# Distances in ScalarE's pauses, grid ahead of the second norm, experts ahead of the x transposes, another order of loads

## The chip, the cores and the metric

One core of a Trainium2 chip. The metric is the device time of one execution in microseconds. Three runs of the kernel before took 381.7, 383.23 and 385.96 us (median 383.23). Engines in this text: TensorE (PE; its weight loads PEld), VectorE (DVE), ScalarE (ACT), GpSimd (POOL) and SyncE (SP), which here only issues DMAs.

## The reference

Input x is 16 images of 256 tokens with 128 channels, in float32. Cut to what matters:

```
mod = silu(c) @ wmod                       # 16 x 6 x 128: sa, ca, ga, sb, cb, gb per image
h   = layernorm(x) * (1 + ca) + sa
# deformable attention: per token 8 heads x 33 taps
wave   = silu(h @ wave_w.T + wave_b)       # gives a frequency and a phase per token
w      = silu(h @ kernel_w.T + kernel_b)   # 8 heads x 33 weights
pos    = clip(l + s * freq + phase, 0, 255)          # s = -16 .. 16
out    = sum_s w[s] * (linear interpolation of h at pos[s])
x   = x + ga * silu(out @ out_w.T)
h   = layernorm(x) * (1 + cb) + sb
# experts: the two best of 8 by h @ router_w.T + router_b, not weighted
x   = x + gb * (sum of the two chosen experts' h @ expert_w[e] + expert_b[e])
```

The gates ga and gb are kept at least 0.25 away from zero.

## The kernel before, in words

The 16 images are cut into nine units: image 0 alone, seven units of two images, image 15 alone. A unit of two images is four tiles of 128 tokens. Each engine has its program written out by hand: a loop over i = -2 to 7, in which each pass works on several units at once, and after it a hand-written tail for the last two units (LATE is unit 7, LAST is unit 8). Engines meet only through semaphores; each engine runs its list strictly in order.

One pass i does this:

- **front of unit i+1**. ScalarE normalises x (norm1, one pass earlier), TensorE transposes it (front_xT), ScalarE applies the modulation (front_hT), TensorE multiplies with the 297 projection columns (front_row), ScalarE writes silu into the table T (front_row) and takes two tanh (front_wave). VectorE turns these into a line per token (`line`, L616 to L624) and into the weights of the ends (`ends_of`, `products`). ScalarE spreads the line over 50 grid columns (front_u, L422 and L429), and VectorE makes from it the shift masks and `near`, the distance of each grid column from its tap (`grid`, L648 to L660).
- **middle of unit i**. VectorE shifts T by six predicated copies (`network`, L673). ScalarE turns `near` into the interpolation weights c: six Abs of 172 columns each, one for each offset within a block (front_c, L439), then one Relu (L442). VectorE multiplies T by c into the dense attention matrix AT (`spread_out`, L705, two instructions for each image). TensorE transposes AT in 8 groups for each image (mid_A, L879), ScalarE copies each group out of PSUM (mid_A, L453), and TensorE multiplies with h (mid_attend, L893). The second image of unit i gets its mid_A in the next pass. Then come aoT, the output projection, silu, gate, and VectorE adds to x (`residual`, L724).
- **back of unit i-1**. ScalarE sums squares (stats2, L348), GpSimd makes the reciprocal root in three small dependent operations (rstd2, L306, L308, L310), ScalarE normalises (norm2, L362), TensorE transposes (back_x2T, L919), ScalarE modulates (back_h2T, L484), TensorE makes logits (L929), VectorE picks the two best (`route`, L733 to L749), and the masks go out to DRAM and come back spread over all partitions (two DMAs of SyncE).
- **end of unit i-2**. VectorE multiplies h by the masks (`masked`, L766, one instruction an image), TensorE multiplies with the 8 experts (back_experts, L967, one call an image), ScalarE scales (back_moe, L500), TensorE transposes back, VectorE adds to x (`total`), SyncE stores.

What sets the order around the change is the list of each engine. ScalarE's runs: front_hT, mid_A of the second image, mid_ao, mid_y, mid_gate, the rows of T, front_wave, front_hs, front_c, stats2, norm2, front_u, back_h2T, back_moe, mid_A of the first image, back_mk, norm1 (L503 to L521). VectorE's runs: network 0 and 1, stats1, sum_ends, network 2 and 3, masked of image 0, network 4, masked of image 1, residual, network 5, line, ends_of, spread_out of image 0, grid, route, spread_out of image 1, products, total (L776 to L799). TensorE's is at L976 to L998: there the first image's experts are multiplied ahead of the transposes of x, and the second image's behind them.

At the start ScalarE's queue issues cT, the whole of wmod, the biases and the projection weights, SyncE's queue the rest. VectorE splits the biases into three bf16 parts and sums them on three partitions (parts_on_partitions), then copies all modulation out of PSUM.

## Time and profile before

| | |
|---|---|
| median of three runs | 383.23 us (381.7 to 385.96) |
| the profiled execution's own time | 380.88 us |
| its span, first to last instruction | 379.1 us |
| PE busy | 269.6 us (71%) |
| PEld busy | 185.9 us (49%) |
| DVE busy | 287.3 us (76%) |
| ACT busy | 218.4 us (58%) |
| POOL busy | 55.8 us (15%) |
| mean granted TensorE clock | 0.86 of full speed |
| DMA | 12.91 MB, mean 34 GB/s |

The profiled execution is 2.35 us below the median of the three runs, and its own time is 1.78 us above its span. Busy shares are averages over a start (to 38.2 us), seven long passes of the loop (to 320.05 us) and a tail (59.05 us); the stretches are cut where VectorE begins the shifts of a unit.

### The profile page before, as it was taken

The page shows a single profiled execution, that of the slowest core. Times are in us where ns is not written, and L with a number is a line of the kernel's source. Part 1 is how long each engine was busy: PE and PEld are TensorE (multiplying, and loading weights), DVE is VectorE, ACT ScalarE, POOL GpSimd, SP SyncE. Part 2 cuts the span into 40 slices and gives each one's busy share as a digit, 9 for nine tenths or more (in the row PEclk, how much of TensorE's full clock was granted, in tenths as well). Part 3 has the DMA queues.
Part 4 walks back from the last instruction along what each step waited for, and adds up shares of the span by engine and source line. Part 5 has one row for each costly group of instructions (what it writes and reads, how often), then busy time and mean ns, then how long its engine had stood idle before and what let it go on. Part 6 is the DMA issues. An engine that isn't in the chain of part 4 may idle for free.

```text
span 379.1 us, 5072 instructions
## 1 busy us (share of the span) xinstructions
PE 269.6 (71%) x1720; PEld 185.9 (49%) x1720; DVE 287.3 (76%) x650; ACT 218.4 (58%) x539; POOL 55.8 (15%) x64
## 2 busy tenths in 40 slices
PE   6745815894598749890988639892898388779796
PEld 2324404543464537560764427551664266357574
DVE  6699996997499846997299954998299949950723
ACT  2573665856576846774486744854576546565301
POOL 5110231112102030205002140114000300001100
PEclk9686975999589969997699958997699979889889
DMA  7600000200012000400022000400013002200001
GB/s 223 160 2 0 2 0 0 58 0 0 3 27 100 0 1 2 139 3 0 0 83 59 0 0 2 141 2 0 1 44 97 1 2 56 85 0 3 28 0 42
DMA packets 11871, 12.91 MB, mean 34 GB/s; under 512 B 1139, under 2 KB 10694, under 8 KB 11078
## 3 DMA queue, kind: packets, MB, share of 16 engines
q1 hardware_dynamic: 11108, 12.05, 10.6%
q10 hardware_dynamic: 738, 0.55, 0.6%
q8 instruction: 13, 0.21, 0.2%
q14 instruction: 12, 0.10, 0.1%
HBM read 10.45 MB, written 2.15 MB: 33 GB/s over the span
## 4 chain that ended last, share of the span: by engine, by line
PE 47%; ACT 27%; DVE 10%; POOL 8%; issue 7%; DMA 1%; SPq 0%; ACTq 0%; POOLq 0%; DVEq 0%
PE pT L879 12%; PE pE L967 12%; ACT A L453 6%; PE pR L859 5%; POOL rs L308 5%; ACT xn L362 5%; PE pY L893 4%; ACT c L439 4%; DVE T L673 3%; ACT xn L348 3%; DVE AT L705 2%; PE pL L929 2%; PE pY L903 2%; POOL ve L306 2%; ACT hT L383 2%
## 5 line engine op out<-in xcount | busy, mean ns | idle before, releaser
L879 PE MATMUL pT<-early,AT 128*128 128x128 f32 x512 | 78.6, 301 | 21.9 <-ACT A L453 11.6
L453 ACT ACTIVATE A<-pT 128x512 f32<-128x512 f32 x128 | 71.2, 596 | 30.2 <-PE pT L879 30.2
L673 DVE COPY_PREDICATED T<-mask,T 128x672 f32<-128x672 int16 (+11 forms) x54 | 82.9, 1534 | 1.0
L879 PEld LDWEIGHTS pT<-early,AT 128*128 128x128 f32 x512 | 61.3, 154 | 36.8 <-ACT A L453 23.6
L705 DVE TENSOR_TENSOR AT<-T,c 128x2064 f32<-128x2064 f32 x32 | 72.3, 2302 | 2.8 <-ACT c L442 2.8
L967 PE MATMUL pE<-hm,late 128*128 128x256 f32 x240 | 66.8, 440 | 0.0
L967 PEld LDWEIGHTS pE<-hm,late 128*128 128x128 f32 x240 | 52.3, 224 | 10.9 <-issue 1.3
L306 POOL TENSOR_SCALAR ve<-sq 128x4 f32<-128x4 f32 (+1 forms) x18 | 9.7, 538 | 295.0 <-ACT xn L348 159.0
L919 PE MATMUL pX<-early,xn 128*128 128x128 f32 x32 | 8.4, 407 | 62.1 <-ACT xn L362 62.1
L362 ACT ACTIVATE xn<-x,nm,rs 128x128 f32<-128x128 f32 x64 | 26.4, 480 | 34.9 <-POOL nm L310 34.9
L919 PEld LDWEIGHTS pX<-early,xn 128*128 128x128 f32 x32 | 5.3, 202 | 65.1 <-ACT xn L362 65.0
L893 PE MATMUL pY<-A,hs 128*32 128x256 f32 x512 | 32.2, 394 | 0.0
L766 DVE TENSOR_TENSOR hm<-mkb,h2T 128x2048 f32<-128x2048 bf16 x13 | 29.6, 2278 | 0.0
L308 POOL TENSOR_TENSOR rs<-ve,mhalf 128x4 f32<-128x4 f32 (+1 forms) x18 | 28.9, 1603 | 1.5
L859 PE MATMUL pR<-proj,hT 128*128 128x297 f32 x64 | 25.7, 485 | 0.8 <-ACT hT L383 0.8
L500 ACT ACTIVATE moeT<-pE,modT 128x256 f32<-128x256 f32 x15 | 6.3, 471 | 28.2 <-PE pE L967 28.2
L648 DVE SCALAR_TENSOR_TENSOR eI<-uR,early 128x200 int16<-128x200 f32 (+1 forms) x9 | 3.1, 344 | 24.6 <-ACT uR L429 24.4
L893 PEld LDWEIGHTS pY<-A,hs 128*32 128x32 f32 x512 | 15.4, 113 | 12.3 <-ACT A L453 3.1
L395 ACT ACTIVATE T<-pR 128x297 f32<-128x297 f32 x32 | 13.6, 424 | 13.4 <-PE pR L859 13.4
L439 ACT ACTIVATE c<-near,early 128x172 f32<-128x172 f32 (+1 forms) x54 | 20.1, 542 | 0.0
L733 DVE TENSOR_TENSOR lg<-pL,rb 128x32 f32<-128x32 f32 (+1 forms) x9 | 1.7, 187 | 23.3 <-PE pL L929 23.2
L724 DVE SCALAR_TENSOR_TENSOR x<-pY,x 128x128 f32<-128x128 f32 x32 | 7.5, 289 | 14.7 <-PE pY L909 14.7
(129 smaller groups left out, 359.4 us busy)
## 6 DMA issues: line engine op xcount, KB each, us to landing
mkb<-mask_rows SPq DMA_DIRECT2D x6, 1024.0 KB, 5.2
x<-in_x SPq DMA_DIRECT2D x7, 256.0 KB, 7.5
out<-x SPq DMA_DIRECT2D x7, 256.0 KB, 5.0
late<-in_late SPq DMA_DIRECT2D x1, 592.0 KB, 5.5
mkb<-mask_rows SPq DMA_DIRECT2D x1, 512.0 KB, 5.1
wmod<-in_wmod ACTq DMA_DIRECT2D x1, 384.0 KB, 4.1
early<-in_early SPq DMA_DIRECT2D x1, 278.0 KB, 4.3
x<-in_x SPq DMA_DIRECT2D x2, 128.0 KB, 3.6
```

What stands on the lines that cost most here:

```text
L306: nc.gpsimd.tensor_scalar(ve[:, 0:w], sq[:, 0:w], 1.0 / C, EPS, ALU.mult, ALU.add).then_inc(done, 1)
L308: nc.gpsimd.tensor_tensor(rs[:, 0:w], ve[:, 0:w], mhalf[:, 0:w], ALU.pow).then_inc(out, 1)
L362: ins = nc.scalar.activation(xn[:, bt, :], of_x(n)[:, bt, :], ACT.Identity, bias=nm[:, bt:bt + 1], scale=rs[:, bt:bt + 1])
L439: ins = nc.scalar.activation(cells[:, :, :, r], near[:, 0:w, :], ACT.Abs, bias=off[:, r:r + 1])
L453: nc.scalar.activation(A[b][:, m, 2 * j:2 * j + 2, :].rearrange("p h l -> p (h l)"), pT[k % 2][:, :], ACT.Copy).then_inc(a_A, 1)
L673: nc.vector.copy_predicated(rows[:, :, :, j0:j1], spread(mask[:, k, 0:w, j0:j1], [P, w, H, j1 - j0], 2), rows[:, :, :, j0 + (1 << bit):j1 ...
L705: nc.vector.tensor_tensor(AT[:, bt, :, :].rearrange("p h (j r) -> p h j r", r=BLK), spread(T[n % 2][:, bt, 0:H, 0:NB], [P, H, NB, BLK], 3) ...
L766: nc.vector.tensor_tensor(hm[b][:, :, :], mkb[n % 2][:, :, b * L:(b + 1) * L], spread(own, [P, E, L], 1), ALU.mult).then_inc(v_hm, 1)
L859: mm(dst, hT[:, bt * P:(bt + 1) * P], proj[:, :], start=False, stop=True).then_inc(t_row, 1)
L879: ins = nc.tensor.transpose(pT[k % 2][:, c0:c0 + P], AT[:, 2 * b + i, 2 * j + a, m * P:(m + 1) * P], ident)
L893: ins = mm(pY[32 * j:32 * j + 32, b * L:(b + 1) * L], hs[n % 2][:, 2 * b + m, hh, :], A[b][:, m, hh, :], start=(m == 0 and a == 0), stop=( ...
L967: ins = mm(dst, weT[:, e, :], hm[b][:, e, :], start=False, stop=(e == E - 1))
```

## The change

- ScalarE: front_c is cut into its six Abs, which go one, one, one and three at a time between the pieces of the front and of the middle, and the Relu (front_fall) between the last two rows of T. The second image's mid_A moves ahead of front_hT, stats2 ahead of front_hs, and front_u ahead of norm2.
- TensorE: the first half of the second image's mid_A moves ahead of front_xT; front_row comes between the pieces of the middle; the second image's experts move ahead of back_x2T.
- VectorE: residual moves ahead of the second masked; the expert biases are prepared one pass earlier, the gates one pass later.
- Start: ident gets a load of its own, the projection weights move to SyncE's queue, wmod comes in two parts and so does the modulation; the loads of x from unit 2 on and of the late weights wait until the first front_hT has run.
- Tail: the lists of all engines are ordered anew; the first image's masked of unit 6 goes ahead of spread_out of unit 8, and its experts ahead of mid_gate of unit 7.

The diff, cut to its core:

```diff
@@ -259,13 +260,20 @@
                 sp.dma_start(of_x(n), rows_of("x", n)).then_inc(d_x[n], 16)
 
             load_x(0)
+            sp.dma_start(packs["first"][:, :], t["first"]).then_inc(d_first, 16)
+            sp.dma_start(proj[:, 0:NW], t["proj"][:, 0:NW]).then_inc(d_proj, 16)
+            sp.dma_start(proj[:, NW:NW + H], t["proj"][:, NW:NW + H]).then_inc(d_proj, 16)
+            sp.dma_start(proj[:, NW + H:NW + 2 * H], t["proj"][:, NW + 32:NW + 40]).then_inc(d_proj, 16)
+            load_x(1)
             sp.dma_start(packs["early"][:, :], t["early"]).then_inc(d_early, 16)
             sp.dma_start(bits[:, :, :], t["bits"].rearrange("p (k j) -> p k j", j=NGRID)).then_inc(d_bits, 16)
-            load_x(1)
             sp.dma_start(packs["experts"][:, :], t["experts"]).then_inc(d_exp, 16)
+
+            sp.wait_ge(a_hT, 1)
+            load_x(2)
             sp.dma_start(packs["late"][:, :], t["late"]).then_inc(d_late, 16)
             sp.dma_start(rb[:, :], t["rb"].rearrange("(a e) -> a e", a=1).to_broadcast([P, E])).then_inc(d_late, 16)
-            for n in range(2, NU):
+            for n in range(3, NU):
                 load_x(n)
 
             def masks(n):
...
@@ -328,16 +336,14 @@
         @block.scalar
         def _(act):
             act.dma_start(cT[:, :], t["cT"]).then_inc(d_c, 16)
-            act.dma_start(wmod[:, :], t["wmod"]).then_inc(d_wmod, 16)
+            act.dma_start(wmod[:, 0:2 * C], t["wmod"][:, 0:2 * C]).then_inc(d_wmod[0], 16)
             act.dma_start(kbl[:, 0:NW], t["kbl"].to_broadcast([NP, NW])).then_inc(d_kb, 16)
             wvb = t["wvb"].rearrange("r a -> a r")
             act.dma_start(kbl[:, NW:NW + H], wvb[:, 0:H].to_broadcast([NP, H])).then_inc(d_kb, 16)
             act.dma_start(kbl[:, NW + H:NW + 2 * H], wvb[:, 32:32 + H].to_broadcast([NP, H])).then_inc(d_kb, 16)
             act.wait_ge(d_c, 16)
             nc.scalar.activation(scT[:, :], cT[:, :], ACT.Silu).then_inc(a_silc, 1)
-            act.dma_start(proj[:, 0:NW], t["proj"][:, 0:NW]).then_inc(d_proj, 16)
-            act.dma_start(proj[:, NW:NW + H], t["proj"][:, NW:NW + H]).then_inc(d_proj, 16)
-            act.dma_start(proj[:, NW + H:NW + 2 * H], t["proj"][:, NW + 32:NW + 40]).then_inc(d_proj, 16)
+            act.dma_start(wmod[:, 2 * C:6 * C], t["wmod"][:, 2 * C:6 * C]).then_inc(d_wmod[1], 16)
 
             def squares(n, junk, total, mu, meant, count, sq, done):
 
...
@@ -428,17 +434,21 @@
                     act.wait_ge(v_sc, n)
                 nc.scalar.activation(uR[:, 0:tiles(n), :], u[:, 0:tiles(n), :], ACT.Copy, bias=ROUND).then_inc(a_uR, 1)
 
-            def front_c(n):
+            def front_c(n, r0, r1):
 
                 w = tiles(n)
-                act.wait_ge(v_near, n + 1)
-                if n > 0:
-                    act.wait_ge(v_mult, LT * before(n))
+                if r0 == 0:
+                    act.wait_ge(v_near, n + 1)
+                    if n > 0:
+                        act.wait_ge(v_mult, LT * before(n))
                 cells = c[:, 0:w, :].rearrange("p a (j r) -> p a j r", r=BLK)
-                for r in range(BLK):
-                    ins = nc.scalar.activation(cells[:, :, :, r], near[:, 0:w, :], ACT.Abs, bias=off[:, r:r + 1])
-                ins.then_inc(a_abs, 1)
-                act.wait_ge(a_abs, n + 1)
+                for r in range(r0, r1):
+                    nc.scalar.activation(cells[:, :, :, r], near[:, 0:w, :], ACT.Abs, bias=off[:, r:r + 1]).then_inc(a_abs, 1)
+
+            def front_fall(n):
+
+                w = tiles(n)
+                act.wait_ge(a_abs, BLK * (n + 1))
                 nc.scalar.activation(c[:, 0:w, :], c[:, 0:w, :], ACT.Relu, bias=1.0, scale=-1.0).then_inc(a_c, 1)
 
             def mid_A(n, b, halves=(0, 1)):
...
@@ -501,41 +513,47 @@
                                          scale=scale_of(5, n, b)).then_inc(a_moe, 1)
 
             for i in range(-2, LAST):
+                second(i, -1, mid_A, 1)
                 run(i, 1, front_hT)
-                second(i, -1, mid_A, 1)
+                run(i, 0, front_c, 0, 1)
                 run(i, -1, mid_ao)
+                run(i, 0, front_c, 1, 2)
+                run(i, 1, front_row, 0)
+                run(i, 0, front_c, 2, 3)
                 run(i, -1, mid_y)
                 run(i, -1, mid_gate)
-                run(i, 1, front_row, 0)
                 run(i, 1, front_row, 1)
+                run(i, 0, front_c, 3, BLK)
+                run(i, 1, front_row, 2)
+                run(i, 0, front_fall)
+                run(i, 1, front_row, 3)
                 run(i, 1, front_wave)
+                run(i, -1, stats2)
                 run(i, 1, front_hs)
-                run(i, 0, front_c)
-                run(i, -1, stats2)
+                run(i, 1, front_u)
                 run(i, -1, norm2)
-                run(i, 1, front_u)
                 run(i, -1, back_h2T)
                 run(i, -2, back_moe)
                 run(i, 0, mid_A, 0)
                 run(i, -1, back_mk)
                 run(i, 2, norm1)
-            mid_A(LATE, 1, (0,))
-            front_c(LAST)
-            mid_A(LATE, 1, (1,))
+            mid_A(LATE, 1)
+            front_c(LAST, 0, BLK)
             mid_ao(LATE)
+            front_fall(LAST)
             mid_y(LATE)
             mid_gate(LATE)
             mid_A(LAST, 0)
             stats2(LATE)
             mid_ao(LAST)
-            norm2(LATE)
             mid_y(LAST)
             mid_gate(LAST)
+            norm2(LATE)
             back_h2T(LATE)
             back_moe(LATE - 1)
             stats2(LAST)
+            norm2(LAST)
             back_mk(LATE)
-            norm2(LAST)
             back_h2T(LAST)
             back_mk(LAST)
             back_moe(LATE)
...
@@ -566,25 +588,35 @@
                 nc.vector.memset(T[0][:, :, :, :], 0.0).then_inc(v_zero, 1)
 
             def projection_parts():
-                dve.wait_ge(d_early, 16)
                 dve.wait_ge(d_kb, 48)
                 dve.wait_ge(g_zero, 3)
-                parts_on_partitions(kbl[:, :], kbr[:, :], kbs, kbt, kbp[:, :], ident[0:NP, 0:NP], v_kbp)
+                parts_of(kbl[:, :], kbr[:, :], kbs, v_kbp)
+
+            def projection_rows():
+                dve.wait_ge(d_first, 16)
+                on_partitions(kbs, kbt, kbp[:, :], ident[0:NP, 0:NP], v_kbp)
 
             def expert_parts():
                 dve.wait_ge(d_exp, 16)
-                parts_on_partitions(eb, ebr[:, :], ebs, ebt, ebp[:, :], pmask, v_ebp)
+                parts_of(eb, ebr[:, :], ebs, v_ebp)
+                on_partitions(ebs, ebt, ebp[:, :], pmask, v_ebp)
+
+            def selectors():
                 nc.vector.tensor_copy(sel[:, :, :], spread(ident[0:NP * E, 0:E], [NP * E, E, P], 2)).then_inc(v_ebp, 1)
 
-            def modulation():
-                dve.wait_ge(t_mod, 1)
-                nc.vector.tensor_copy(modT[:, :, :].rearrange("p k b -> p (k b)"), pR[0][:, 0:6 * B]).then_inc(v_modT, 1)
-                dve.wait_ge(v_modT, 1)
-                nc.vector.tensor_scalar(modT[:, 1:5:3, :], modT[:, 1:5:3, :], 1.0, None, ALU.add).then_inc(v_modT, 1)
+            def modulation(part):
+
+                ks = slice(0, 2) if part == 0 else slice(2, 6)
+                dve.wait_ge(t_mod, part + 1)
+                nc.vector.tensor_copy(modT[:, ks, :].rearrange("p k b -> p (k b)"),
+                                      pL[:, ks.start * B:ks.stop * B]).then_inc(v_modT, 1)
+                dve.wait_ge(v_modT, 2 * part + 1)
+                nc.vector.tensor_scalar(modT[:, 3 * part + 1, :], modT[:, 3 * part + 1, :], 1.0, None, ALU.add).then_inc(v_modT, 1)
 
             def gates():
 
                 gate = modT[:, 2:6:3, :]
+                dve.wait_ge(v_modT, 3)
                 nc.vector.tensor_scalar(gsT[:, :, :], gate, 0.0, 2.0, ALU.is_ge, ALU.mult)
                 nc.vector.scalar_tensor_tensor(gaT[:, :, :], gate, -1.0, gate, ALU.mult, ALU.max).then_inc(v_gate, 1)
                 dve.wait_ge(v_gate, 1)
...
@@ -773,19 +807,21 @@
                                         ALU.add).then_inc(v_out, 1)
 
             start()
-            for i in range(-2, LAST):
+            stats1(0)
+            projection_parts()
+            modulation(0)
+            projection_rows()
+            for i in range(-1, LAST):
                 run(i, 0, network, range(0, 2))
                 run(i, 2, stats1)
-                if i == -2:
-                    projection_parts()
-                    modulation()
-                    gates()
+                if i == -1:
+                    expert_parts()
                 run(i, 0, sum_ends)
                 run(i, 0, network, range(2, 4))
                 run(i, -2, masked, 0)
                 run(i, 0, network, range(4, 5))
+                run(i, -1, residual)
                 second(i, -2, masked, 1)
-                run(i, -1, residual)
                 run(i, 0, network, range(5, 6))
                 run(i, 1, line)
                 run(i, 1, ends_of)
...
@@ -796,11 +832,13 @@
                 run(i, 1, products)
                 run(i, -2, total)
                 if i == 0:
-                    expert_parts()
+                    modulation(1)
+                    gates()
+                    selectors()
             network(LAST, range(0, 6))
             sum_ends(LAST)
+            masked(LATE - 1, 0)
             spread_out(LAST, 0)
-            masked(LATE - 1, 0)
             residual(LATE)
             masked(LATE - 1, 1)
             residual(LAST)
...
@@ -825,11 +863,14 @@
             pe.wait_ge(v_zero, 1)
             warm_up(9)
             pe.wait_ge(a_silc, 1)
-            pe.wait_ge(d_wmod, 16)
-            for k in range(6):
-                ins = mm(pR[0][:, k * B:(k + 1) * B], wmod[:, k * C:(k + 1) * C], scT[:, :], start=True, stop=True)
-            ins.then_inc(t_mod, 1)
-            pe.wait_ge(d_early, 16)
+            def modulation(part, ks):
+                pe.wait_ge(d_wmod[part], 16)
+                for k in ks:
+                    ins = mm(pL[:, k * B:(k + 1) * B], wmod[:, k * C:(k + 1) * C], scT[:, :], start=True, stop=True)
+                ins.then_inc(t_mod, 1)
+
+            modulation(0, range(0, 2))
+            pe.wait_ge(d_first, 16)
 
             def front_xT(n):
                 pe.wait_ge(a_xn1, n + 1)
...
@@ -974,21 +1015,24 @@
                 ins.then_inc(t_out, 1)
 
             for i in range(-2, LAST):
+                second(i, -1, mid_A, 1, 0)
                 run(i, 1, front_xT)
-                second(i, -1, mid_A, 1, 0)
                 second(i, -1, mid_A, 1, 1)
                 second(i, -1, mid_attend, 1, 0)
                 second(i, -1, mid_attend, 1, 1)
+                run(i, 1, front_row, 0)
                 run(i, -1, mid_y)
-                run(i, 1, front_row, 0)
+                run(i, 1, front_row, 1)
                 run(i, -1, mid_gate)
-                run(i, 1, front_row, 1)
+                run(i, 1, front_row, 2, 3)
+                if i == -1:
+                    modulation(1, range(2, 6))
                 run(i, 1, front_hb)
                 if i == -1:
                     warm_up(9)
                 run(i, -2, back_experts, 0)
+                second(i, -2, back_experts, 1)
                 run(i, -1, back_x2T)
-                second(i, -2, back_experts, 1)
                 run(i, -1, back_logits)
                 run(i, 0, mid_A, 0, 0)
                 run(i, -2, back_out)
```

The hunks left out declare the semaphores, make back_h2T and back_logits of unit 0 wait for the second part of the modulation, split parts_on_partitions into parts_of and on_partitions, move the wait for `early` to line(0), and reorder TensorE's tail: there back_experts(LATE - 1, 0) moves from behind mid_attend(LAST, 0, 1) to between mid_y(LATE) and mid_gate(LATE), and back_experts(LATE - 1, 1) from behind back_x2T(LATE) to before it.

## Rows read from the trace of the kernel before

**Rows 1.** Busy us by stretch: length, PE, PEld, DVE, ACT, POOL, granted clock, DMA share, GB/s.

```profile
196.96:240.80 43.84, 31.71 (x210) 22.26 (x209) 34.11 (x75) 26.47 (x66) 7.64 (x6) 0.84 0.09 30
...
320.05:379.10 59.05, 47.60 (x277) 34.06 (x274) 28.91 (x67) 24.28 (x60) 2.70 (x6) 0.88 0.11 34
```

**Rows 2.** VectorE's waits between 38.2 and 320.05: us in total, times, longest.

```profile
DVE eI L648 <- ACT uR L429: 24.0, 6, 4.2
DVE lg L733 <- PE pL L929: 22.9, 6, 5.1
DVE AT L705 <- ACT c L442: 2.8, 2, 2.0
```

**Rows 3.** Order of time, VectorE, one pass: start, us, instruction, idle before in brackets.

```profile
209.86 2.28 DVE L766 TENSOR_TENSOR hm<-mkb,h2T 128x2048 f32<-128x2048 bf16 x1
...
212.90 1.80 DVE L673 COPY_PREDICATED T<-mask,T 128x1376 f32<-128x1376 int16 x1
...
215.31 0.16 DVE L624 SCALAR_TENSOR_TENSOR nlf<-lp,invf 128x4 f32<-128x4 f32 x1
...
216.39 4.52 DVE L705 TENSOR_TENSOR AT<-T,c 128x2064 f32<-128x2064 f32 x2
...
225.45 0.37 DVE L648 SCALAR_TENSOR_TENSOR eI<-uR,early 128x200 int16<-128x200 f32 x1 [4.18 <-ACT uR L429]
...
232.29 0.19 DVE L733 TENSOR_TENSOR lg<-pL,rb 128x32 f32<-128x32 f32 x1 [5.00 <-PE pL L929]
```

**Rows 4.** Order of time, ScalarE, the same pass.

```profile
211.55 2.40 ACT L439 ACTIVATE c<-near,early 128x172 f32<-128x172 f32 x6
213.98 1.06 ACT L442 ACTIVATE c<-c 128x1032 f32<-128x1032 f32 x1
...
222.09 1.65 ACT L362 ACTIVATE xn<-x,nm,rs 128x128 f32<-128x128 f32 x4 [5.28 <-POOL nm L310]
223.64 1.37 ACT L422 ACTIVATE u<-early,nlf,invf 128x50 f32<-128x50 f32 x4
...
225.32 1.00 ACT L484 ACTIVATE h2T<-pX,modT 128x256 f32<-128x256 f32 x2
...
232.84 1.09 ACT L453 ACTIVATE A<-pT 128x512 f32<-128x512 f32 x2 [0.44 <-PE pT L879]
...
238.35 1.63 ACT L362 ACTIVATE xn<-x,nm,rs 128x128 f32<-128x128 f32 x4
```

**Rows 5.** Order of time, TensorE, the same pass.

```profile
210.71 3.72 PE L967 MATMUL pE<-hm,late 128*128 128x256 f32 x16
223.79 1.12 PE L919 MATMUL pX<-early,xn 128*128 128x128 f32 x4 [9.36 <-ACT xn L362]
...
225.16 6.30 PE L967 MATMUL pE<-hm,late 128*128 128x256 f32 x16
231.30 0.95 PE L929 MATMUL pL<-late,h2T 128*128 128x8 f32 x8
```

**Rows 6.** Order of time, GpSimd, that pass and a later one.

```profile
216.97 1.77 POOL L306 TENSOR_SCALAR ve<-sq 128x4 f32<-128x4 f32 x1 [12.72 <-ACT xn L348]
218.83 2.95 POOL L308 TENSOR_TENSOR rs<-ve,mhalf 128x4 f32<-128x4 f32 x1
...
299.90 1.10 POOL L308 TENSOR_TENSOR rs<-ve,mhalf 128x4 f32<-128x4 f32 x1
```

**Rows 7.** VectorE's waits up to 38.2.

```profile
DVE kbs L548 <- DMA early<-in_early: 1.7, 1, 1.7
```

**Rows 8.** Order of time, ScalarE, the start.

```profile
9.74 0.56 ACT L383 ACTIVATE hT<-pX,modT 128x256 f32<-128x256 f32 x1 [2.65 <-DVE modT L583]
```

**Rows 9.** Order of time, VectorE, the start: first of eight operations for expert biases.

```profile
35.66 0.21 DVE L548 CAST ebs<-experts 24x128 bf16<-24x128 f32 x1
```

**Rows 10.** Order of time, ScalarE, the tail.

```profile
354.44 0.59 ACT L493 ACTIVATE mkT<-pL 24x512 bf16<-24x512 f32 x1 [1.77 <-PE pL L935]
```

**Rows 11.** Order of time, VectorE, the first spread_out of a later pass.

```profile
300.63 4.52 DVE L705 TENSOR_TENSOR AT<-T,c 128x2064 f32<-128x2064 f32 x2
```

More of the change, by code:

```diff
@@ L74 @@
 PACKS = {
-    "early": (P, [("ident", P), ("xrow", NGRID), ("jcol", BT * NGRID), ("off", BLK), ("ends", BT * 2 * END),
+    "first": (P, [("ident", P)]),
+    "early": (P, [("xrow", NGRID), ("jcol", BT * NGRID), ("off", BLK), ("ends", BT * 2 * END),
                   ("sign", BT * 2), ("edge", BT * 2), ("lcol", BT)]),
@@ L167, in build @@
         pL = bank("pL")
[L169 removed]
+        d_c = sem("d_c"); d_wmod = [sem(f"d_wmod{i}") for i in range(2)]; d_first = sem("d_first"); d_early = sem("d_early"); d_late = sem("d_late"); d_kb = sem("d_kb")
         d_proj = sem("d_proj"); d_bits = sem("d_bits"); d_exp = sem("d_exp")
@@ L384, in front_hT, with front_row @@
                                          bias=scale_of(0, n, b), scale=scale_of(1, n, b)).then_inc(a_hT, 1)
-            def front_row(n, b):
-                for bt in range(LT * b, min(LT * (b + 1), tiles(n))):
+            def front_row(n, *own):
+                for bt in (q for q in own if q < tiles(n)):
                     g = LT * before(n) + bt
@@ L545, in _, with parts_of @@
         def _(dve):
-            def parts_on_partitions(x_, rest, parts, sums_, out, of_part, done):
+            def parts_of(x_, rest, parts, done):
                 nc.vector.tensor_copy(parts[:, 0, :], x_).then_inc(done, 1)
@@ L842, in front_xT, with front_row @@
                 ins.then_inc(t_xT, 1)
-            def front_row(n, b):
-                for bt in range(LT * b, min(LT * (b + 1), tiles(n))):
+            def front_row(n, *own):
+                for bt in (q for q in own if q < tiles(n)):
                     g = LT * before(n) + bt
                     if g == 0:
-                        pe.wait_ge(v_modT, 1)
                         pe.wait_ge(v_kbp, 7)
@@ L1003, in _ @@
             mid_y(LATE)
+            back_experts(LATE - 1, 0)
             mid_gate(LATE)
```

13 lines of the change are left out of this document (9 added, 4 removed).

## The prediction

> **What bounds the kernel now.** I first cut the span where VectorE starts the shifts of a unit. A full pass of the loop takes 43.84 us and holds 34.11 us of VectorE, 31.71 of TensorE and 26.47 of ScalarE [rows 1]. No engine is full, so the order is the bound. VectorE's waits show where: between 38.2 and 320.05 us it waited 24.0 us for uR, 22.9 for the logits and 2.8 for c [rows 2], 49.7 us in all. The order of time in one pass shows why: VectorE runs without a gap from the start of the pass at 196.96 to the end of the first spread_out near 221.3 (225.45 less the wait), waits 4.18 us for the grid's input and, 1.84 us of grid later (232.29 - 5.00 - 225.45), 5.00 us for the logits [rows 3]. The line `nlf` that ScalarE needs for the grid is ready at 215.47 [rows 3], but ScalarE stands in norm2 and waits for GpSimd until 222.09; u and its rounding run from 223.64 to 225.32 [rows 4]. So the grid waits for a norm that it does not need. The logits wait for the same norm (x transposes at 223.79, behind 9.36 us of idle TensorE) and then for the second image's experts, 6.30 us between the x transposes and the logits [rows 5].
>
> GpSimd is late for two reasons. Its chain starts only at 216.97, since ScalarE does the six Abs (2.40 us) and the Relu (1.06) first [rows 4, 6]. And its small operations stand still while VectorE runs a large one: `ve` took 1.77 us from inside the first AT product, `rs` 2.95 from inside the second, ending 0.9 us after it; an `rs` that began at 299.90, among VectorE's small operations, took 1.10 [rows 3, 6].
>
> **The loop, step by step**, in the clock times of this pass, with VectorE unbroken from 196.96.
>
> *Residual* ran in the 0.76 us between the end of the second masked (212.14) and network 5 (212.90) [rows 3]. Ahead of masked, which takes 2.28, it ends near 210.7. VectorE's sum is unchanged, and `nlf` stays at 215.5. ScalarE's stats2 took from the Relu's end (215.04) to 216.97, so 1.9 us [rows 4, 6]; it now ends near 212.6 if ScalarE is free.
>
> *The Abs and the Relu* add no work: 3.46 us move. Their cover is ScalarE's waits in the first half. Of its 17.4 us without work (43.84 - 26.47 [rows 1]) 5.28 lie before norm2 [rows 4] and about as much behind the experts, at most 6.30 [rows 5]; some 6 remain for attend, output projection and rows, and I take 3 of them as usable. That covers most; what isn't covered delays the second tanh by at most 1 us against a need of `line` near 214.6. If the cover is gone the cost is 3.46 us on ScalarE, not on VectorE. front_hT moves into the wait for attend.
>
> *GpSimd.* `ve` then stands in masked (to 212.9 in the new order), `rs` in network 5 (to 214.7) and ends 0.9 us later at 215.6; nm is there at 216. It must begin before the AT products at 216.39, or it waits for the first of them (2.3 us).
>
> *u ahead of norm2*: 215.5 to 217.2 (1.68 us). *norm2* 217.2 to 218.85. The second image's *experts*: masked ends at 212.9, so the two calls (3.72 us each after busy stretches [rows 5]) end by 220 at worst and, by the start of the first call at about 211, by 218.7. *x transposes* 0.7 to 1.1, *h2T* 1.0, *logits* 0.95 at most [rows 4, 5]: they end between 221.4 and 222.
>
> *VectorE*: the grid follows the first spread_out at 221.3, with its input four microseconds old, so no wait. The route is due at 223.1, with logits 1 to 1.7 us before it: no wait. The pass becomes 43.84 - 4.18 - 5.00 = 34.66 us, VectorE's own 34.11 plus its issue gaps. Late next would be the logits; then ScalarE: from its first copy of A (232.84) to the end of norm1 (239.98) are 7.14 us [rows 4]. The first copy now comes at about 222.6 (behind logits), so norm1 ends at 229.8, just as the second spread_out ends; the next copies need that and 0.7 us more. ScalarE has 0.7 us to spare there, and 3 us at the residual. SyncE's mask transfers start earlier with mkT and are no nearer to their user.
>
> Over the loop the waits of 49.7 us go, at most. I give back 3 us for places where a unit's slack runs out (seven passes at 0.4): **-47**. Bounds: none of the small slacks holds, 14 us given back; or nothing given back.
>
> **The start.** VectorE waited 1.7 us for `early` before the bias parts [rows 7], and ScalarE's first hT waited 2.65 us for the modulation behind them [rows 8]. Now the parts need only the biases, the modulation comes in between, and the sums after it. hT gains up to 2.65. The first projection still follows all seven bias operations and now two of the modulation too, at 0.2 us each (the smallest in [rows 3] are 0.16 and 0.19): 1.7 - 0.4, about 1.2. The projection's loads leave SyncE's queue earlier but now share the first microseconds with fewer bytes of wmod. From 0 (loads land no earlier) to 2.5. The expert biases (seven operations, with the selectors' one from 35.66 to 38.2, 2.5 us [rows 9]) move ahead of the first line, where VectorE has nothing else. At the mean of 0.32 us the seven are 2.2; six small ones of modulation and gates, put at 0.2 to 0.3 each, take their place: 0.7 us gained. The held back loads of x are needed 10 us after their issue; cost nothing, or, if unit 2 lands late, 2 us. Sum **-2**, from +1 to -3.5.
>
> **The tail** (59.05 us [rows 1]). A call of 16 expert products, 3.72 us at the full clock [rows 5], leaves the stretch between the last attend and the x transposes of unit 7. Against that, mid_gate of unit 7 waits for the first of them (2.3 us later than it could), and the last spread_out comes behind a masked (2.28 us); since ScalarE's copies of unit 7 are no longer split by front_c, the last transposes still start about 1 us earlier. norm2(LAST) ahead of back_mk(LATE) costs 0.8 us. Walking the lists, mkT of unit 7 comes 3 us earlier than its 354.44 - 320.05 = 34.4 us after the stretch begins [rows 10]; behind it nothing changes. **-3**, from +1 to -6.
>
> Sum: 380.88 - 47 - 2 - 3 = 328.9 us for an execution like the profiled one. The median lay 2.35 us above it: **331 us**.
>
> **A rule against it.** The rows show that GpSimd waits for VectorE's large two-input instructions. They show no wait the other way: the AT products at 300.63 began while `rs` of 299.90 ran, and took 4.52 us like those of [rows 3] [rows 6, 11]. The Trainium skill (SBUF — State Buffer, "SBUF: two separate sides") calls the pair of ports that the two share an exclusive lock: whichever instruction starts first has it whole, and the other blocks. By that rule VectorE, now unbroken, would stand for each GpSimd operation that slips in first.
>
> **Rivals.**
> (a) *The small slacks fail*: nm misses 216.39, or the logits come 1 to 2 us late, in each of seven passes: 7 to 14 us back, 335 to 345. For: nm has 0.2 to 0.4 us. Against: even nm at 218.9 moves the logits to 223.5 only. 0.17.
> (b) *GpSimd is shut out*: if `rs` is let in neither behind masked nor behind network 5, it ends after the first spread_out, near 222. norm2 ends at 224, the logits at 227 with slower transposes: VectorE waits 4 us in each of 7 passes, 28 less the 3 given back: 356. Against: `ve` of 216.97 was let in between two back-to-back products [rows 6]. 0.06.
> (c) *VectorE stands for GpSimd*: an exclusive hold would cost VectorE three operations of 0.2, 1.0 and 0.2 us a pass, 1.4 x 7 = 10 us: 341. This is what the rule quoted above would do here. Against it stand the products at 300.63 [rows 11]. 0.05.
> (d) *Slower: TensorE's granted clock.* A pass holds 31.71 us of TensorE at 0.84 of the full clock [rows 1], 26.6 at full. It is not granted fully, and drops after idle stretches (3.72 us against 6.30 for the same products [rows 5]). If work packed closer were granted less, TensorE would be the bound: at 1.2 GHz (0.5) a pass would be 53 us, 9.4 more than now in each of seven: 449. It decides against the change below 26.6 / 43.84 = 0.61. Against: the tail, busy for 47.60 of 59.05 us, was granted 0.88, the pass, busy for 31.71 of 43.84, 0.84 [rows 1]. 0.02.
> (e) *It does more*: nothing given back and a better clock in the tail, 320 to 324. 0.07.
> (f) *It doesn't do what it says*: ScalarE, now with 0.7 us to spare, becomes the bound and its copies of A start late, about 4 us a pass: 356, like (b). 0.04.
>
> **How the numbers follow.** My forecast (324 to 336) has 0.59. 331 is its middle, a little to the late side. The range 322 to 345 leaves out (b), (f), (d) and half of (e), and half of (c) may stand at its edge; some 0.83 is in it. A change under 1% could not be told from none in this kernel. All cases but (d) lie over 1% below 383.23, so faster 0.96; for a cause that I do not see, both others get the rest: same 0.02, slower 0.02.
>
> **What would show it.** Right: passes of 34.5 to 35.5 us; no entry of VectorE for uR or logits over 1 us in total a pass; u ahead of norm2's end; the second experts at 3.7 us, not 6.3; `rs` ending near 18.7 us after the pass begins. Wrong: VectorE's wait at lg of 2 us or more (a, b); AT products or shifts longer than 4.52 and 1.80 us (c); TensorE rows at 1.5 times their length throughout (d); waits of TensorE for A copies that stand behind norm1 (f).

## The result: 327 us, the loop shorter by 48.7 us

The changed kernel took 326.8 us (median of four runs, 326.45 to 327.7) against 383.26 for the one before (four runs): a ratio of 0.8524, 95% interval 0.8473 to 0.8575. The profiled execution took 327.7 us, with a span of 325.9. The forecast was 331.

| | before | after |
|---|---|---|
| span of the profiled execution | 379.1 us | 325.9 us |
| start, to VectorE's first shift of unit 1 | 38.20 | 36.12 |
| loop, seven passes | 281.85 | 233.16 |
| tail | 59.05 | 56.62 |
| a middle pass | 43.84 | 34.5 |
| VectorE busy | 287.3 (76%) | 286.1 (88%) |
| TensorE busy | 269.6 (71%) | 266.9 (82%) |
| mean granted clock | 0.86 | 0.895 |

The engines do the same work; what went is idle time. One pass of the changed kernel and its tail, cut as in [rows 1], with the same columns:

```profile
169.08:203.64 34.56, 30.29 (x196) 22.15 (x200) 33.96 (x74) 25.58 (x64) 5.75 (x6) 0.90 0.13 38
...
269.28:325.90 56.62, 46.28 (x285) 32.84 (x281) 29.01 (x67) 23.65 (x60) 2.52 (x6) 0.91 0.12 35
```

A pass of 34.56 us holds 33.96 of VectorE: it is now the bound. The granted clock rose with the packing, 0.84 in [rows 1] and 0.90 here. What is left of VectorE's waits, over the whole span (us in total, times, longest):

```profile
DVE x L758 <- PE pY L949: 10.1, 1, 10.1
DVE hm L794 <- PE pT L987: 9.2, 3, 4.6
DVE lg L767 <- PE pL L970: 4.1, 3, 1.6
...
DVE eI L682 <- ACT uR L435: 0.8, 1, 0.8
```

The entry for uR, 24.0 us in [rows 2], is 0.8, once, in the start. Of the 4.1 us for the logits, 22.9 in [rows 2], only 1.6 lie in the loop. The large ones left, x and hm, lie in the tail, as they did before.

One pass of the changed kernel, which begins at 169.08, in order of time. VectorE:

```profile
185.06 1.81 DVE L707 COPY_PREDICATED T<-mask,T 128x1376 f32<-128x1376 int16 x1
...
188.61 4.52 DVE L739 TENSOR_TENSOR AT<-T,c 128x2064 f32<-128x2064 f32 x2
...
193.39 0.36 DVE L682 SCALAR_TENSOR_TENSOR eI<-uR,early 128x200 int16<-128x200 f32 x1
...
195.14 0.18 DVE L767 TENSOR_TENSOR lg<-pL,rb 128x32 f32<-128x32 f32 x1
```

No bracket stands behind eI (4.18 us in [rows 3]) nor behind lg (5.00). ScalarE:

```profile
180.38 1.05 ACT L452 ACTIVATE c<-c 128x1032 f32<-128x1032 f32 x1
...
187.70 1.38 ACT L428 ACTIVATE u<-early,nlf,invf 128x50 f32<-128x50 f32 x4 [2.33 <-DVE nlf L658]
...
189.39 1.63 ACT L368 ACTIVATE xn<-x,nm,rs 128x128 f32<-128x128 f32 x4
191.77 1.02 ACT L496 ACTIVATE h2T<-pX,modT 128x256 f32<-128x256 f32 x2 [0.75 <-PE pX L959]
```

The Relu is done 12.4 us into the pass (18.1 in [rows 4]), u comes before norm2, and norm2 no longer waits 5.28 us for GpSimd. GpSimd:

```profile
185.05 1.84 POOL L314 TENSOR_SCALAR ve<-sq 128x4 f32<-128x4 f32 x1 [8.64 <-ACT xn L354]
186.97 1.01 POOL L316 TENSOR_TENSOR rs<-ve,mhalf 128x4 f32<-128x4 f32 x1
188.06 0.20 POOL L318 TENSOR_TENSOR nm<-mu,rs 128x4 f32<-128x4 f32 x1
```

`ve` was held up (1.84 us) by the shift of 185.06, `rs` ran free at 1.01 where [rows 6] had 2.95. `nm` ends at 188.26, 0.35 us before the first AT product at 188.61. TensorE:

```profile
185.43 3.72 PE L1008 MATMUL pE<-hm,late 128*128 128x256 f32 x16
191.08 0.66 PE L959 MATMUL pX<-first,xn 128*128 128x128 f32 x4 [1.93 <-ACT xn L368]
192.85 1.40 PE L970 MATMUL pL<-late,h2T 128*128 128x8 f32 x8 [1.11 <-ACT h2T L496]
194.10 3.81 PE L919 MATMUL pT<-first,AT 128*128 128x128 f32 x16
```

The second experts are finished before the x transposes, at 3.72 us and not the 6.30 of [rows 5], and the x transposes wait 1.93 us and not 9.36. The low clock has not gone, it has moved: the 16 transposes of A behind the logits were granted 0.50 and took 3.81 us, where the kernel before needed 1.07 to 1.14 for eight of them (at 232.11 and 233.49). VectorE waits for none of them.

Not every pass had that 0.35 us. In the second of the seven, which begins at 66.37, `rs` started only 0.04 us before the AT products, and `nm` met the first of them:

```profile
83.58 1.01 POOL L316 TENSOR_TENSOR rs<-ve,mhalf 128x4 f32<-128x4 f32 x1
84.67 1.33 POOL L318 TENSOR_TENSOR nm<-mu,rs 128x4 f32<-128x4 f32 x1
```

```profile
83.62 4.53 DVE L739 TENSOR_TENSOR AT<-T,c 128x2064 f32<-128x2064 f32 x2
...
91.87 0.19 DVE L767 TENSOR_TENSOR lg<-pL,rb 128x32 f32<-128x32 f32 x1 [1.62 <-PE pL L970]
```

`nm` ended 2.38 us after the products began, and the logits came 1.62 us late: this is the 1.6 us of the loop.

Start and tail, each by a ScalarE row of the changed kernel: the first hT, which came at 9.74 after 2.65 us of waiting [rows 8], and mkT of unit 7, which came 34.4 us after the tail's beginning [rows 10] and now 31.8.

```profile
8.14 0.56 ACT L389 ACTIVATE hT<-pX,modT 128x256 f32<-128x256 f32 x1 [0.65 <-PE pX L882]
```

```profile
301.07 0.59 ACT L505 ACTIVATE mkT<-pL 24x512 bf16<-24x512 f32 x1 [0.15 <-PE pL L976]
```

### The profile page after: what moved, and what is told of

Read it like the earlier page. It is cut to its first block, busy times and chain, and to the rows that moved or that the text cites. A ratio compares the mean times of both kernels' runs of the same rounds, so it can differ in the third digit from the quotient of the medians.

```text
span 325.9 us, 5078 instructions
## 1 busy us (share of the span) xinstructions
PE 266.9 (82%) x1720; PEld 185.7 (57%) x1720; DVE 286.1 (88%) x652; ACT 217.6 (67%) x539; POOL 44.0 (13%) x64
## 4 chain that ended last, share of the span: by engine, by line
DVE 48%; PE 23%; issue 16%; ACT 10%; POOL 2%; ACTq 0%; DVEq 0%; POOLq 0%
DVE T L707 14%; DVE AT L739 13%; PE pT L919 7%; DVE hm L800 4%; PE pE L1008 4%; ACT A L463 3%; PE pR L899 2%; PE pL L970 2%; ACT xn L368 1%; DVE prodN L719 1%; DVE x L758 1%; DVE topi L775 1%; DVE endw L727 1%; PE pY L933 1%; DVE st L632 1%
## 5 line engine op out<-in xcount | busy, mean ns | idle before, releaser
L919 PE MATMUL pT<-first,AT 128*128 128x128 f32 x512 | 83.3, 316 | 18.2 <-DVE AT L749 10.6
L919 PEld LDWEIGHTS pT<-first,AT 128*128 128x128 f32 x512 | 66.0, 162 | 34.4 <-ACT A L463 17.2
L1008 PE MATMUL pE<-hm,late 128*128 128x256 f32 x240 | 57.4, 394 | 0.0
L1008 PEld LDWEIGHTS pE<-hm,late 128*128 128x128 f32 x240 | 45.5, 195 | 7.8 <-issue 0.2
L316 POOL TENSOR_TENSOR rs<-ve,mhalf 128x4 f32<-128x4 f32 (+1 forms) x18 | 19.9, 1104 | 1.5
L428 ACT ACTIVATE u<-early,nlf,invf 128x50 f32<-128x50 f32 x32 | 11.2, 417 | 11.3 <-DVE nlf L658 11.3
L959 PE MATMUL pX<-first,xn 128*128 128x128 f32 x32 | 6.3, 320 | 13.8 <-ACT xn L368 13.8
L970 PE MATMUL pL<-late,h2T 128*128 128x8 f32 x60 | 9.6, 285 | 8.3 <-ACT h2T L496 8.3
L970 PEld LDWEIGHTS pL<-late,h2T 128*128 128x128 f32 x60 | 8.9, 225 | 10.5 <-ACT h2T L496 9.4
L318 POOL TENSOR_TENSOR nm<-mu,rs 128x4 f32<-128x4 f32 (+1 forms) x18 | 14.3, 797 | 1.4
```

The source lines that it names most:

```text
L316: nc.gpsimd.tensor_tensor(rs[:, 0:w], ve[:, 0:w], mhalf[:, 0:w], ALU.pow).then_inc(out, 1)
L919: ins = nc.tensor.transpose(pT[k % 2][:, c0:c0 + P], AT[:, 2 * b + i, 2 * j + a, m * P:(m + 1) * P], ident)
L970: ins = mm(pL[:, bt * E:(bt + 1) * E], h2T_of(n)[:, bt * P:(bt + 1) * P], rwT, start=True, stop=True)
L1008: ins = mm(dst, weT[:, e, :], hm[b][:, e, :], start=False, stop=(e == E - 1))
```

## The experiments

Twelve kernels ran. The same 383 us kernel stood beside them each time, at medians of 383.9 to 385.1; ratios are to it.

**The two exchanges alone, on the kernel before.** First ScalarE's u ahead of norm2:

```
# ScalarE's loop
+    run(i, 1, front_u)
     run(i, -1, norm2)
-    run(i, 1, front_u)
```

> The kernel before with one exchange: ScalarE's u (grid input) ahead of norm2. Theory (the order of one pass): u then fits into ScalarE's wait for GpSimd, so VectorE's wait of 4.18 us for uR goes, but the logits come when they came (norm2 still starts with nm, the second experts still stand between the x transposes and the logits), so the wait for the logits grows by as much: about 9 us a pass, total unchanged, 380 to 385 us. Rival (each wait has its own worth): 24 us less, 359.

Measured: 385.64 us, ratio 1.0017 (0.9964 to 1.0069). VectorE's waits in this kernel:

```profile
DVE lg L733 <- PE pL L929: 48.8, 9, 9.4
```

The wait for uR is gone (0.5 us left) and the whole of it has come back at the logits: 48.8 us over the whole span, 47.5 of them in the loop, where [rows 2] had 22.9. Two waits in a row for one cause, the late norm2, and taking away the first pays nothing.

Then the second image's experts ahead of the x transposes:

```
# TensorE's loop
+    second(i, -2, back_experts, 1)
     run(i, -1, back_x2T)
-    second(i, -2, back_experts, 1)
```

> The kernel before with one exchange: the second image's experts ahead of the x transposes on TensorE. Theory: the experts then run in TensorE's 9.4 us of idleness, logits follow h2T by 1 us, near 227.3 in the pass that began at 196.96, just when the grid ends: the wait for the logits falls from 22.9 to under 5 us in all, the wait for uR stays at 24; 361 us (359 to 365). Rival: the logits are held by the norm, not by the experts; under 5 us gained.

Measured: 376.38 us, 0.9781 (0.972 to 0.9843): faster by 7.6 us, a third of the gain that I expected. VectorE's waits, TensorE's order in one pass, and the stretches from its x transposes on (columns as in [rows 1]):

```profile
DVE eI L648 <- ACT uR L429: 27.9, 8, 4.2
...
DVE AT L705 <- ACT c L442: 9.1, 7, 2.0
```

```profile
216.56 3.72 PE L967 MATMUL pE<-hm,late 128*128 128x256 f32 x16
224.50 1.01 PE L919 MATMUL pX<-early,xn 128*128 128x128 f32 x4 [4.21 <-ACT xn L362]
227.09 1.88 PE L929 MATMUL pL<-late,h2T 128*128 128x8 f32 x8 [1.58 <-ACT h2T L484]
228.82 3.81 PE L879 MATMUL pT<-early,AT 128*128 128x128 f32 x16
```

```profile
224.50:228.80 4.30, 2.72 (x12) 2.32 (x13) 1.80 (x5) 3.23 (x9) 0.00 (x0) 0.52 0.01 4
228.80:232.60 3.80, 3.80 (x18) 3.43 (x19) 3.46 (x16) 1.79 (x3) 0.00 (x0) 0.50 0.00 0
```

The experts shrink to 3.72 us, as expected. But TensorE then stands for 4.21 us before the x transposes and is granted 0.52 and 0.50 behind them, the lower of its levels: x transposes 1.01 us (0.66 in the changed kernel), logits 1.88 (1.40), the A transposes 3.81 (as in the changed kernel). In the order before, the experts stood behind the x transposes and were the ones to run slowly in that place [rows 5]. And the AT products now wait for c: ScalarE's copies of A follow the slow transposes, so that its list comes to hT 2.3 us after this pass begins (198.89 and 196.57), where in the kernel before the two fell together (196.89 and 196.96), and the Relu ends 20.4 us into the pass, 18.1 before. In the loop, 15.9 of the 22.9 us at the logits went, but uR took back 3.4 (27.4 and 24.0) and c 5.3 (8.1 and 2.8).

Both together:

> The kernel before with both exchanges, nothing else. Theory: uR in time, logits near 226 against a need at 223.1: 2.9 us of wait a pass are left, 6.3 go; 343 us (339 to 347). If the early GpSimd chain of the changed kernel were not needed at all: 335 or less. Rival (each alone adds up, and u alone is worth 0): as the experts alone, 361.

Measured: 375.47 us, 0.9748 (0.9665 to 0.9831); I had expected 343. The view shows why. GpSimd's chain and ScalarE's norm2 in one pass:

```profile
216.11 0.52 POOL L306 TENSOR_SCALAR ve<-sq 128x4 f32<-128x4 f32 x1 [14.95 <-ACT xn L348]
216.71 2.95 POOL L308 TENSOR_TENSOR rs<-ve,mhalf 128x4 f32<-128x4 f32 x1
219.74 0.59 POOL L310 TENSOR_TENSOR nm<-mu,rs 128x4 f32<-128x4 f32 x1
```

```profile
220.36 1.65 ACT L362 ACTIVATE xn<-x,nm,rs 128x128 f32<-128x128 f32 x4 [2.73 <-POOL nm L310]
```

norm2 still waits for `nm`, and the logits come 5.31 us late in the middle passes: of the 49.7 us of [rows 2], 41.8 are left, 34.4 at the logits and 7.4 at c. The exchanges remove what stands behind the norm, not what makes the norm late. They are worth 8 us without the rest of the change.

**The rest of the change without the exchanges.** In the changed kernel both are undone:

```
# ScalarE's loop
+    run(i, -1, norm2)
     run(i, 1, front_u)
-    run(i, -1, norm2)
# TensorE's loop
+    run(i, -1, back_x2T)
     second(i, -2, back_experts, 1)
-    run(i, -1, back_x2T)
```

> The changed kernel with both exchanges undone (u behind norm2, second experts behind the x transposes); Abs spread, residual early, new start and tail kept. Theory: nm now comes 19 us after the pass begins, norm2 to 20.6, u to 22.4, before the grid is due at 24.3: no wait for uR. x transposes at 20.7, experts to 25.1, logits 26.1, due at 26.1: 0 to 1 us a pass. 327 to 334 us. Rival (the two exchanges carry the gain): 370 or more.

Measured: 343.68 us, 0.8897 (0.8812 to 0.8982), between the two. TensorE's order in one pass and its experts' stretch:

```profile
196.97 1.11 PE L959 MATMUL pX<-first,xn 128*128 128x128 f32 x4 [4.68 <-ACT xn L368]
...
198.33 5.84 PE L1008 MATMUL pE<-hm,late 128*128 128x256 f32 x16
204.01 0.95 PE L970 MATMUL pL<-late,h2T 128*128 128x8 f32 x8
```

```profile
198.33:204.00 5.67, 5.67 (x17) 4.68 (x17) 3.80 (x9) 1.17 (x3) 0.00 (x0) 0.62 0.01 3
```

Spreading the distances, the early residual, start and tail bring some 40 us by themselves. GpSimd is in time in all passes of two-image units but one (there `rs` took 2.95 us and uR came 4.17 us late). The rest hangs on the experts: behind 4.68 us of idle TensorE they are granted 0.62 and take 5.84 us, where I had counted 3.72; the logits come 2.80 us late. Each exchange undone alone tells the two apart:

> The changed kernel with the second image's experts behind the x transposes again. Theory, with the lower clock counted this time: TensorE idles for 5.9 us before the x transposes (22 us after the pass begins), which then take 1.1, the experts 5.8, the logits 0.9: 30 against a need at 26.1, some 4 us of wait a pass, 27 in all: 350 to 356. That is slower than the kernel with both exchanges undone (343.7), since there norm2 doesn't wait for u. Rival (the experts' products at 3.72, as I priced them before): 335. Rival (worth what it was alone in the kernel before, 2.2%): 334.

Experts behind, u ahead: 344.31 us, 0.896 (0.8888 to 0.9032), below the 350 to 356 that I expected. The logits come 1.57 us late in the second pass and 2.75 to 4.35 in the five behind it. The exchange of the experts is worth 17.5 us here. The time is the same as with both undone, so u without the experts gains nothing; the kernel with both undone even had its one pass with a late `rs`, and its other passes were up to 1.5 us shorter than here.

> The changed kernel with u behind norm2 again. Theory: once GpSimd's chain is early (nm 19.2 us after the pass begins), norm2 and u both end 22.5 us after it, before the grid is due at 24.3; nothing is late. 326 to 329 us. Rival (u ahead of norm2 took VectorE's wait for uR away by itself): 20 us slower or more, 347.

u behind, experts ahead: 330.89 us, 0.8621 (0.8553 to 0.869). The profiled execution (329.22) shows five passes of the changed kernel's length, one shorter by 1.25 us, and behind it one of 36.3 (33.7 there), in which `rs` was caught:

```profile
82.62 3.10 POOL L316 TENSOR_TENSOR rs<-ve,mhalf 128x4 f32<-128x4 f32 x1
```

```profile
82.56 4.52 DVE L739 TENSOR_TENSOR AT<-T,c 128x2064 f32<-128x2064 f32 x2
```

It is the same second pass in which the changed kernel's `rs` had started 0.04 us before the products; here it started 0.06 us behind their start, and VectorE waited 3.09 us for uR and 1.00 for the logits. The median is 4 us above the changed kernel's, the profile explains 1.5 of them, and the intervals overlap: what u ahead of norm2 is worth stays open between nothing and 4 us.

**What makes the norm early.** In the changed kernel, c in one piece behind front_wave and the residual behind the second masked:

```
# ScalarE's loop                       # VectorE's loop
-    run(i, 0, front_c, 0, 1)  ...          run(i, 0, network, range(4, 5))
-    run(i, 0, front_fall)             -    run(i, -1, residual)
     run(i, 1, front_wave)                  second(i, -2, masked, 1)
+    run(i, 0, front_c, 0, BLK)        +    run(i, -1, residual)
+    run(i, 0, front_fall)
```

> The changed kernel with the six Abs and the Relu in one piece behind the tanh, and residual behind the second masked. Theory: stats2 ends 18.1 us after the pass begins instead of 15.9, GpSimd's ve and rs still fit between VectorE's small operations, nm is caught by the first AT product (2.3 us); logits 0.5 to 1 us late. 329 to 336 us. Rival (these two brought GpSimd forward, so without them the chain is as late as in the kernel before): 350 or more.

Measured: 358.44 us, 0.9335 (0.9236 to 0.9435): 32 us lost by moving work that has cover. The two moves were not tried one by one. GpSimd's order in two passes of this one execution, then VectorE's:

```profile
166.49 1.59 POOL L314 TENSOR_SCALAR ve<-sq 128x4 f32<-128x4 f32 x1 [12.93 <-ACT xn L354]
168.16 2.95 POOL L316 TENSOR_TENSOR rs<-ve,mhalf 128x4 f32<-128x4 f32 x1
171.19 0.59 POOL L318 TENSOR_TENSOR nm<-mu,rs 128x4 f32<-128x4 f32 x1
...
205.57 1.01 POOL L316 TENSOR_TENSOR rs<-ve,mhalf 128x4 f32<-128x4 f32 x1
206.66 1.33 POOL L318 TENSOR_TENSOR nm<-mu,rs 128x4 f32<-128x4 f32 x1
```

```profile
165.73 4.52 DVE L736 TENSOR_TENSOR AT<-T,c 128x2064 f32<-128x2064 f32 x2
...
177.65 0.19 DVE L764 TENSOR_TENSOR lg<-pL,rb 128x32 f32<-128x32 f32 x1 [5.31 <-PE pL L967]
...
205.63 4.52 DVE L736 TENSOR_TENSOR AT<-T,c 128x2064 f32<-128x2064 f32 x2
...
213.41 0.19 DVE L764 TENSOR_TENSOR lg<-pL,rb 128x32 f32<-128x32 f32 x1 [1.16 <-PE pL L967]
```

Both kinds of pass stand side by side. In one, `rs` starts 0.06 us before the AT products (205.57 and 205.63), takes 1.01, and the logits come 1.16 us late. In the other, `ve` starts 0.76 us behind their start and loses the first product, `rs` loses the second (2.95 us), `nm` meets one more VectorE instruction and ends only at 171.78, 6.05 us after the products began, and the logits come 5.31 us late. Five passes of this execution had an `rs` of 2.95, with waits at the logits of 5.31 (four) and 5.65 us; the pass of the one-image unit lay between the two kinds (`rs` 2.64, logits 2.24 late).

> The changed kernel with front_xT and front_hT ahead of the second image's mid_A again, on both engines. Theory: ScalarE's copies of A start 1.3 us later, residual has 3 us of slack, stats2 slips by under 1 us and ve is caught by network 5 anyway: no cost, 326 to 329. Rival (ScalarE closes the cycle: its 0.7 us before the copies are gone, and each pass is longer by 0.6 us or more): 331 to 336.

The one remaining move in ScalarE's order (front_hT, with TensorE's front_xT, ahead of the second mid_A again):

```
# ScalarE's loop                       # TensorE's loop
+    run(i, 1, front_hT)               +    run(i, 1, front_xT)
     second(i, -1, mid_A, 1)                second(i, -1, mid_A, 1, 0)
-    run(i, 1, front_hT)               -    run(i, 1, front_xT)
```

Measured: 332.06 us (332.0 to 332.49), 0.8646 (0.858 to 0.8713). Again the second pass was caught (`ve` 2.27 us, `rs` 2.95, logits 5.31 late); it was 37.9 us long, 4.2 more than in the changed kernel. The pass before it was 1.5 us shorter, the tail 1.0 us longer, the middle passes behind it 34.0 to 34.8 long, up to 0.24 us more than in the changed kernel. So the caught pass is the largest part of the 5 us, and not all of it.

**The cliff by itself.** If the cause is that `rs` misses a start by tenths of a microsecond, holding VectorE back until `nm` is done must make the slow kernel faster, although it only adds a wait:

```
# VectorE's loop, on the kernel of 358.44 us
+    if i > 0:
+        dve.wait_ge(g_nm2, i)
     run(i, 0, spread_out, 0)
```

> The kernel of b5 (Abs and Relu in one piece, residual behind the second masked; 358.4 us) with one wait more: VectorE starts the first AT product of a pass only when GpSimd's nm is done. In b5 five of six full passes had rs caught by both AT products (rs 2.95 us, 5.31 us of wait at the logits, passes of 38.5 to 39.9 us) and one had rs in before them (1.01 and 1.16, pass 35.8). Theory (the first AT product shuts GpSimd out, and that alone makes the 5.31): rs takes 1.0 in each pass, VectorE pays 1 to 2 us at the new wait and gets over 4 back at the logits; passes near 36 us, 338 to 346 us in all, faster although only a wait was added. Rival (stats2 is late anyway, and a wait only adds to it): 360 or more.

Measured: 337.13 us (336.05 to 338.02), 0.878 (0.8712 to 0.8847): 21.3 us faster by an added wait. VectorE's waits:

```profile
DVE AT L736 <- POOL nm L318: 10.8, 7, 3.5
...
DVE lg L764 <- PE pL L969: 2.4, 2, 1.4
```

It pays 10.8 us in seven waits for `nm` and saves 30.3 at the logits (32.7 before, now 2.4). Every `rs` of a two-image unit took 1.01 to 1.12 us. Nothing else was changed, so the missed start made 21 of the 32 us that this order had lost; the 10 left are about what VectorE now waits for the late norm. Whether the same wait would help the kernel of 383 us, or the changed kernel as it stands, was not tried.

**A better version.** VectorE is the bound, so its smallest movable work, three copies of the end columns of AT (0.42 us an image), goes to ScalarE:

```
# ScalarE, at the head of mid_A: new ends_in(n, b); VectorE's spread_out loses the same three copies
+    act.wait_ge(v_mult, LT * (img + 1)); act.wait_ge(v_endw, n + 1)
+    nc.scalar.activation(AT[:, 2 * b, :, 0:L:L - 1]..., endw[:, 2 * b, :, :], ACT.Copy)
+    ...                                # the two columns of tile 2 * b + 1; increments v_end
# VectorE, ahead of the sums of the end columns, for n > 0
+    dve.wait_ge(v_end, before(n))
```

> The changed kernel with the end columns of AT copied by ScalarE instead of VectorE (three small copies an image, about 0.42 us of VectorE each time). Theory (VectorE's own work is the pass): passes shorter by up to 0.85 us, 7 passes, 6 us: 320 to 323. Rival (ScalarE had 0.7 us to spare before its copies of A; it now has none, stats2 slips behind the line, and rs is caught by the AT products in some passes, 4 us each): 330 to 350.

Measured: 328.44 us (327.94 to 329.78), 0.8564 (0.8515 to 0.8614), not faster than the changed kernel. Five passes became 0.5 to 2.2 us shorter; the second was caught (`rs` 2.95, 37.3 us). With the wait of the experiment before added to it:

> As d1, with VectorE's wait for nm ahead of the first AT product. Theory: passes that were caught in d1 cost a fraction of a us instead of 4; 320 to 324 us, at or below d1 and below the changed kernel (326.8). If ScalarE's order is the bound by then, 327 to 332 with ScalarE without a pause from the copies of A on.

Measured: **323.81 us** (323.0 to 325.36, six runs), 0.8442 (0.8391 to 0.8493). VectorE's waits for logits and `nm`:

```profile
DVE lg L773 <- PE pL L978: 2.4, 2, 1.4
DVE AT L751 <- POOL nm L318: 2.1, 2, 1.5
```

Middle passes of 33.8 to 34.2 us, and no pass caught in the AT products. The added wait is worth 4.6 us here. All six runs lie below the four of the changed kernel (326.45 to 327.7), by about 3 us in the median, and the three passes that took 34.5 us there take 33.9; but the intervals of the two ratios overlap, so that the 3 us are likely and not shown.

**The tail alone.** The changed kernel with the lists behind the loop as they were before:

> The changed kernel with the tail of the kernel before on all engines (front_c of unit 8 between the halves of mid_A of unit 7, masked and experts of unit 6 where they were, norm2 and back_mk as before). Theory: the tail takes 59.05 us again instead of 56.6; 329 to 330 us. Rival (the tail's gain came from the earlier start of its inputs): no change, 327.

Measured: 330.2 us (327.8 to 331.75), 0.859 (0.8535 to 0.8644). The profiled execution's loop was the same, its tail 60.42 us against 56.62. The tail's order is worth about 3 us by this, with intervals that overlap. The order of the loads was not tried by itself.

## Why the prediction was right, and where not

*What bounds.* Right. The two waits of [rows 2] had one cause and went together. The single exchange of u shows it most plainly: one wait removed alone came back whole at the other.

*Residual, Abs and Relu.* Right. stats2 ended 15.8 us into the pass (forecast 15.6), and the moved 3.46 us found their cover: the Relu was done in time for everything.

*GpSimd.* Right in time, wrong in detail. `nm` was forecast at 19.0 us into the pass and ended at 19.2; the AT products began at 19.5. But `ve` stood, where I had expected `rs` to, during network 5, and `rs` ran free.

*Norm, experts, logits.* norm2 ran from 20.3 to 21.9 (forecast 20.2 to 21.9), the experts ended at 20.1 (21.7 to 23.0), the logits at 25.2 (24.4 to 25.0), 0.9 us ahead of their use. The logits themselves took 1.40 us, and not the 0.95 at most of the forecast: TensorE had stood idle for 3.0 of the 3.7 us before them, and they were granted 0.70. The pass took 34.56 us (34.66).

*The sum.* The loop gave 48.7 us (forecast 47: I gave back 3 us, the chip took 1), the start 2.1 (2), the tail 2.4 (3). For an execution like the profiled one that is 327.7 against 328.9. What remains of the 4 us between forecast and median is the 2.35 us that I carried over from the distance of median and profiled execution before; the changed kernel's median lies 0.9 us below its profiled execution, so that this distance does not carry over.

*The rivals' prices.* (c) and (d) are out: the AT products of 83.62 took 4.53 us with `rs` started 0.04 us before them, and the clock rose. (a) came once in the seven passes, as it was priced: in the pass of 66.37 `nm` missed the first AT product (its 2.38 us of delay against the 2.3 forecast), and the logits came 1.62 us late (1 to 2). The wrong step is that (a) stops there: "even nm at 218.9 moves the logits to 223.5 only". That holds when `nm` alone misses its start. When `rs` misses it, `nm` ended 4.57 us after the products began (the second pass with u behind norm2), and when `ve` misses it, 6.05 (the caught pass shown above), which is 222.4 on the prediction's clock. And from the end of `nm` to the end of the logits it was then 5.8 us, not 4.6, since TensorE had idled 5.22 us and was granted 0.50. So a few tenths of a microsecond more turn (a) into the hard case (b), of which I forecast 4 us of wait a pass; it measured 4.1 to 5.65.

That the total was right is partly luck. I had 0.2 to 0.4 us of slack for `nm` and gave rival (b) 0.06. In the second pass `rs` of the changed kernel escaped the products by 0.04 us; with u behind norm2, with hT first and with the end columns on ScalarE (all within 6 us of this kernel) just that pass was caught and took 2.6 to 4.2 us more, and the order with c in one piece was caught in five passes.

*The parts' prices.* I had not split the sum by part, but the expectations show the same error as (a): 361 and 343 us for the exchanges alone against 376 and 375. They counted the work that moved, and neither what an idle TensorE does to the work behind it nor that ScalarE's later copies of A would hold up c (7.4 to 8.1 us in the loop, 2.8 before).

## What to carry to other kernels

Look for one cause behind waits that stand in a row, and price a fix on the last of them: single reorderings here gave 0 and 8 us, the whole change 56. A short chain on GpSimd beside large two-input VectorE instructions needs its start protected, and if slack is a few tenths, an explicit wait on VectorE can be faster than none. When work is taken out of an idle stretch of TensorE, count the next operations at the lower clock.

## What the runs showed of the hardware

- GpSimd's small operations stand still for a whole VectorE instruction, one way only. `rs` took 1.01 us free and 2.95 when it met the second of the two AT products, ending 0.9 us behind it; it took 2.37 to 2.39 when it began 0.24 to 0.26 us into a large shift (in two passes of the changed kernel). VectorE never lengthened: the two AT products took 4.52 or 4.53 us in each case, also when `rs` began 0.04 or 0.06 us before them. The Trainium skill (SBUF — State Buffer, "SBUF: two separate sides") describes a lock that blocks whichever of the two comes second; the rows show this for GpSimd alone.
- The edge is sharp. `rs` that began 0.04 and 0.06 us before the AT products (83.58 and 83.62; 205.57 and 205.63) took 1.01 us, `rs` that began 0.06 us behind their start (82.62 and 82.56) took 3.10. The profile's times on GpSimd are its roughest, so the hundredths are to be read with care; the lengths of 1.01 and 3.10 are far apart. In one execution, `rs` 0.06 us before the products, or `ve` 0.76 us behind their start (166.49 and 165.73), made the difference between 1.16 and 5.31 us of waiting at the logits.
- After 4.2 to 5.2 us of idle, TensorE ran at or near the lower of its two levels in the work that followed (0.52 over 4.30 us and 0.50 over the next 3.80; 0.50 over 3.96; 0.50 over the 1.36 us of the x transposes and 0.62 over the next 5.67), though the mean granted clock of these kernels was 0.84 to 0.88. In the changed kernel's pass, after 1.93 and 1.11 us of idle with 0.66 us of full clock between them, the logits were granted 0.70 and the 3.6 us behind them 0.50.
